# Layer norms by row tile inside the stage that feeds them, and two smaller reorderings, in a two-layer cross-attention kernel on one core

## The chip, the core and the metric

The kernel runs on one core of one Trainium2 chip. Its engines run side by side and are ordered by semaphores alone: TensorE (PE, matrix products), VectorE (DVE), ScalarE (ACT), GpSimd (POOL), and SyncE (SP), whose queue issues all DMAs here. The metric is the device time of one execution in microseconds; lower is better.

## What is computed

Activations `x` of 8 x 112 rows and 512 columns go through two layers, against one context of 8 x 375 rows. All is float32.

```python
# layer 0: 16 heads of 32; layer 1: two attentions of 16 heads of 128, each with one extra key and value
def layer_norm(x, w, b):
    mu = jnp.mean(x, axis=-1, keepdims=True)
    var = jnp.mean(jnp.square(x - mu), axis=-1, keepdims=True)
    return (x - mu) * jax.lax.rsqrt(var + EPS) * w + b
# layer 0
x = x + attention(layer_norm(x, ln1), ctx)            # q, k, v, softmax, output projection
x = x + gelu_tanh(layer_norm(x, ln2) @ fc_w + fc_b) @ proj_w + proj_b      # 512 -> 2048 -> 512
# layer 1
x = x + cross_attention(layer_norm(x, ln1), ctx, ...)  # inner width 2048
x = x + cross_attention(layer_norm(x, ln2), ctx, ...)
x = x + gelu(layer_norm(x, ln_mlp) @ w_fc1 + b_fc1) @ w_fc2 + b_fc2
```

There are five layer norms, here numbered e = 0 to 4: before layer 0's queries (0), before its MLP (1), before the queries of layer 1's two attentions (2 and 3) and before the last MLP (4).

## The kernel before, in words

`x` stays in SBUF as seven row tiles of 128 rows (`RT`). A float32 product is made of three products of halves (`product`, lines 1090 to 1095): every operand is split into a rounded `hi` and a rest `lo`. The normalized and transposed activations are `act_t` (hi and lo). Weights pass through two slots, a and b: a DMA loads a block of 512 x 512 into `w_raw` in four column parts (`load_block`), ScalarE writes the hi part (`split_hi`), GpSimd or VectorE the lo part (`split_lo`), and the next load of a part waits for the lo of the one before.

`schedule` (lines 249 to 275) is the order that every engine follows: norm 0, the first two contexts, queries, attention of layer 0, its projection, norm 1, four MLP blocks, then a hardware loop of two (`a`) with norm 2 + a, contexts, four groups of queries, attention and four groups of projections, then norm 4 and four MLP blocks. Each engine has its own function of each name, and an engine's stream is in order.

**A norm.** The statistics of a row tile are made on VectorE behind the add that finishes it (`add_y`, line 1017, when `last`). `ln_head` (line 834) runs before the add of the last tile: epsilon, one square root on ScalarE for six tiles, reciprocals, normalization (`normalized`, line 829) of tiles 0 and 1 into `prob`. Then `ln` takes the tiles in turn: four transposes on TensorE into one of two PSUM banks (line 1104), scale and bias on ScalarE into one of two `o` buffers (line 596), the two halves on VectorE (lines 861 and 863). Only then come ScalarE's split of the pending weight block (the b slot's block that the previous stage had not split; line 604) and GpSimd's work: it waits for the last half of the last tile (line 502), subtracts the pending block, and adds the bias of the coming projection to `x` (line 507, seven operations), and after that the context halves (line 513).

**Queries** (line 1107): eight tiles per group, t (four column parts) outer and half (448 rows each) inner, into the four banks of `ps_y` in turn; the first tile waits for four row tiles of the norm, the second for all seven. ScalarE writes them into four staging buffers (`staged`: `prob` 0 and 1, `o` 0 and 1), SyncE stores each to a scratch in DRAM, and after each pair loads a part of the block after the next. SyncE's `ln` has the reload of the pending slot ahead of the contexts and of all query stores.

**The MLP** (line 1304): up for rows 0 to 511 and for 512 to 895 (`MLP_CHUNKS`), four tiles of 128 hidden columns each, then down for both, row tile by row tile. **The projection** (line 1282) goes row tile by row tile through the four banks.

## Time and profile before

| what | value |
|---|---|
| median of 3 runs | 2485.12 us (2481.1 to 2485.22) |
| profiled execution, its own time | 2485.79 us |
| its span in the profile | 2484.0 us |
| granted TensorE clock, mean of the span | 0.984 |
| TensorE busy | 2388.7 us (96%) |
| VectorE busy | 1063.9 us (43%) |
| ScalarE busy | 1069.8 us (43%) |
| GpSimd busy | 584.0 us (24%) |
| share of TensorE on the chain that ended last | 81% |

A busy TensorE is not one at its peak: its products are pipelined, and a granted clock of 0.50 means that they run at half speed. A line of the timeline gives the start in microseconds, the length, the engine, the line of the code, the operation, what it writes and reads, its shape, how many were merged into the line, and in brackets the engine's idle time before it with what ended it.

### The profile page before, as it was taken

To read this page: it belongs to the slowest core of one execution; us is meant where nothing else is said; L and a number is where in the kernel's file an instruction comes from. 1 tells how busy PE (TensorE), PEld (TensorE's weight loads), DVE (VectorE), ACT (ScalarE), POOL (GpSimd) and SP (SyncE) were. 2 spreads that over 40 slices of the span, in tenths; PEclk is the share of its full clock that TensorE was granted. 3 is DMA by queue.
4 is the path that set the end of the run, shared out by engine and by line. 5 is a ranking of instruction groups with operands and counts; after the bars stand their busy time and mean duration, and the time that the engine had idled before them with its cause. 6 is when DMAs were issued, how large, how long until landed. Compare 5 with 4: busy or idle time off the path is not lost.

```text
span 2484.0 us, 45212 instructions
## 1 busy us (share of the span) xinstructions
PE 2388.7 (96%) x13858; PEld 2118.2 (85%) x13858; DVE 1063.9 (43%) x2313; ACT 1069.8 (43%) x2551; POOL 584.0 (24%) x975
## 2 busy tenths in 40 slices
PE   6999889999999999999999899999999999999999
PEld 5777678888998998998998798998998998988788
DVE  6777663441333333334334522333333333344633
ACT  3677742243444444444443433444444444452321
POOL 4111023240222222223121230222223122221421
PEclk9999889999999999999999999999999999999999
DMA  6110012244112112112214262113112112215110
GB/s 191 44 34 20 10 48 61 62 131 118 42 57 95 55 44 94 59 49 88 71 58 132 62 187 79 49 50 94 59 42 92 59 61 81 70 51 152 56 51 30
DMA packets 196144, 179.45 MB, mean 72 GB/s; under 512 B 53758, under 2 KB 184242, under 8 KB 196018
## 3 DMA queue, kind: packets, MB, share of 16 engines
q1 hardware_dynamic: 196018, 177.97, 23.4%
q8 instruction: 55, 0.90, 0.2%
q14 instruction: 71, 0.58, 0.1%
HBM read 144.89 MB, written 33.05 MB: 72 GB/s over the span
## 4 chain that ended last, share of the span: by engine, by line
PE 81%; issue 9%; DVE 4%; ACT 3%; POOL 2%; DMA 0%; ACTq 0%; SPq 0%; POOLq 0%; DVEq 0%
PE ps_v L1093 9%; PE ps_v L1095 9%; PE ps_v L1094 9%; PE ps_k L1093 8%; PE ps_k L1095 8%; PE ps_k L1094 8%; PE ps_o L1243 6%; PE ps_s L1093 3%; PE ps_s L1095 3%; PE ps_s L1094 3%; PE ps_o L1093 3%; PE ps_o L1095 3%; PE ps_o L1094 3%; PE ps_t L1232 3%; PE ps_t L1173 1%
## 5 line engine op out<-in xcount | busy, mean ns | idle before, releaser
L513 POOL TENSOR_TENSOR cs_lo<-ctx_raw,cs_hi 128x376 fp32r<-128x376 f32 x288 | 284.5, 1019 | 739.3 <-DVE cs_hi L874 739.3
L969 DVE SCALAR_TENSOR_TENSOR k_lo<-ps_k,col_b,k_hi 128x375 fp32r<-128x375 f32 x256 | 155.6, 608 | 673.2 <-ACT k_hi L696 673.2
L1093 PE MATMUL ps_v<-w_b_hi,cs_hi 128*128 128x512 f32 (+1 forms) x928 | 389.6, 420 | 9.1 <-POOL w_b_lo L497 7.5
L1093 PE MATMUL ps_k<-cs_hi,w_a_hi 128*128 128x376 f32 x1152 | 390.4, 339 | 5.7 <-DVE k_lo L969 4.1
L1095 PE MATMUL ps_k<-cs_hi,w_a_lo 128*128 128x376 f32 x1152 | 385.5, 335 | 0.0
L1094 PE MATMUL ps_k<-cs_lo,w_a_hi 128*128 128x376 f32 x1152 | 385.1, 334 | 0.0
L1095 PE MATMUL ps_v<-w_b_hi,cs_lo 128*128 128x512 f32 (+1 forms) x928 | 365.5, 394 | 0.0
L1094 PE MATMUL ps_v<-w_b_lo,cs_hi 128*128 128x512 f32 (+1 forms) x928 | 365.4, 394 | 0.0
L696 ACT ACTIVATE k_hi<-ps_k,col_b 128x375 fp32r<-128x375 f32 x256 | 146.8, 573 | 423.4 <-PE ps_k L1095 412.3
L713 ACT ACTIVATE prob<-ps_s,row_columns 112x376 f32<-112x376 f32 x256 | 147.1, 574 | 217.9 <-DVE row_columns L975 217.9
L1093 PEld LDWEIGHTS ps_k<-cs_hi,w_a_hi 128*128 128x128 f32 x1152 | 217.2, 189 | 18.9 <-issue 6.2
L1094 PEld LDWEIGHTS ps_k<-cs_lo,w_a_hi 128*128 128x128 f32 x1152 | 217.0, 188 | 10.4
L1095 PEld LDWEIGHTS ps_k<-cs_hi,w_a_lo 128*128 128x128 f32 x1152 | 217.1, 188 | 0.0
L1243 PE MATMUL ps_o<-prob_t,v 128*128 128x112 f32 (+1 forms) x1536 | 211.8, 275 | 0.0
L1243 PEld LDWEIGHTS ps_o<-prob_t,v 128*128 128x128 f32 (+1 forms) x1536 | 209.1, 193 | 0.0
L1095 PEld LDWEIGHTS ps_v<-w_b_hi,cs_lo 128*128 128x128 f32 (+1 forms) x928 | 172.1, 185 | 42.1
L1093 PEld LDWEIGHTS ps_v<-w_b_hi,cs_hi 128*128 128x128 f32 (+1 forms) x928 | 173.5, 187 | 40.3 <-issue 9.6
L625 ACT ACTIVATE v<-ps_v 128x512 f32<-128x512 f32 (+1 forms) x216 | 128.8, 596 | 167.5 <-PE ps_v L1095 167.5
L1094 PEld LDWEIGHTS ps_v<-w_b_lo,cs_hi 128*128 128x128 f32 (+1 forms) x928 | 172.9, 186 | 28.3
L497 POOL TENSOR_TENSOR w_b_lo<-w_raw_b,w_b_hi 128x512 fp32r<-128x512 f32 x84 | 107.6, 1307 | 358.4 <-ACT w_b_hi L582 225.5
L535 POOL CAST k_hi<-xk_hi 128x1 fp32r x256 | 47.8, 187 | 583.7 <-PE ps_s L1095 583.7
L892 DVE TENSOR_SCALAR prob<-prob,row_columns 112x376 f32<-112x376 f32 (+1 forms) x384 | 170.0, 443 | 13.5
(197 smaller groups left out, 4394.0 us busy)
## 6 DMA issues: line engine op xcount, KB each, us to landing
ctx_raw<-in_ctx_t SPq DMA_DIRECT2D x72, 752.0 KB, 5.4
w_raw_a<-in_blocks_a SPq DMA_DIRECT2D x104, 256.0 KB, 3.1
w_raw_b<-in_blocks_b SPq DMA_DIRECT2D x104, 256.0 KB, 3.2
q_lo<-q_scratch SPq DMA_DIRECT2D x72, 224.0 KB, 2.5
o_scratch<-o SPq DMA_DIRECT2D x64, 224.0 KB, 2.0
q_scratch<-prob SPq DMA_DIRECT2D x36, 224.0 KB, 2.6
q_scratch<-o SPq DMA_DIRECT2D x36, 224.0 KB, 2.5
cs_hi<-o_scratch SPq DMA_DIRECT2D x6, 672.0 KB, 4.2
```

Of the source, the lines that this page charges most:

```text
L497: pool.tensor_tensor(w[slot][1][:, :, part], w_raw[slot][:, :, part], w[slot][0][:, :, part], ALU.subtract).then_inc(w_lo[slot], 1)
L513: pool.tensor_tensor(cs[place.parity][1][:, part], ctx_raw[place.parity][:, part], cs[place.parity][0][:, part], ALU.subtract).then_inc(cs ...
L625: act.activation(v[place.parity][0:n, i, :], ps_v[0:n, :], ACT.Identity).then_inc(v_ev, 1)
L696: act.activation(k[t % 2][0][:, 0:LK], ps_k[:, 0:LK], ACT.Identity, bias=col_b[:, ds(place.column((C_BK0, C_BK1), t), 1)]).then_inc(k_hi, 1)
L713: act.activation(prob[buf][0:LQ, 0:KW], ps_s[buf][0:LQ, 0:KW], ACT.Exp, bias=max_neg[0:LQ, buf:buf + 1], accum_out=prob_sum[0:LQ, buf:buf ...
L892: dve.tensor_scalar(p[0:LQ, 0:keys], p[0:LQ, 0:keys], prob_rcp[0:LQ, col:col + 1], None, ALU.mult).then_inc(s_norm, 1)
L969: dve.scalar_tensor_tensor(out=k[t % 2][1][:, 0:LK], in0=ps_k[:, 0:LK], scalar=col_b[:, ds(place.column((C_BK0, C_BK1), t), 1)], in1=k[t % ...
L1093: pe.matmul(out, w_h, m_h, start=first, stop=False)
L1094: pe.matmul(out, w_h, m_l, start=False, stop=False)
L1095: return pe.matmul(out, w_l, m_h, start=False, stop=last)
L1232: last = pe.transpose(ps_t[buf][0:n, i * LQ:(i + 1) * LQ], prob[buf][0:LQ, i * P:i * P + n], ident[0:LQ, 0:LQ])
L1243: last = pe.matmul(ps_o[t % 2][:, 0:LQ], v[place.parity][0:n, i, t * P:(t + 1) * P], prob_t[t % 2][0:n, i * LQ:(i + 1) * LQ], start=(i == ...
```

## The change

Rows pass through the norm while the stage before still runs. Behind a projection (norms 1, 3, 4), the square root, reciprocal and normalization of a row tile follow one row behind the add, the turn of row r - 2 stands behind the products of row r on TensorE, and VectorE's halves stand at the end of each row. Behind the MLP of layer 0 (norm 2), `TURNS_LATE` puts the turns of rows 0 and 1 behind down row 3, of row 2 behind row 4, and so on. In all of them rows 5 and 6 are turned behind the first two tiles of the next stage (the query or the first chunk of up). Queries now go through the first half of the rows with all four column parts, then through the second half, and only tile 4 waits for the whole norm. Normalized rows have buffers of their own (`xhat`). The first norm is done row by row as well, and ScalarE takes over the hi part of the first weight block from GpSimd. On SyncE the pending slot's reload moves from `ln` to behind the fourth query store. ScalarE's split of the pending block moves behind the fourth query tile, or, in the MLP, into the first chunk. Epsilon becomes the bias of the square root. Two inner hardware loops are unrolled (the halves of the query groups, and blocks 0 to 2 of the last MLP).

```diff
@@ -54,6 +54,9 @@
...
+TURNS_LATE = {3: (0, 1), 4: (2,), 5: (3,), 6: (4,)}
@@ -249,29 +253,32 @@
...
-            query(0, 0, 0, 0, A_Q0, 0)
+            query(0, 0, 0, 0, A_Q0, 0, norm=0)
             attend_first()
-            project(0, 0, 0, 1, B_O0, 0, 0)
+            project(0, 0, 0, 1, B_O0, 0, 0, norm=1)
             ln(1, RT)
-            mlp(0, 0, 1, RT)
+            mlp(0, 0, 1, RT, before=1)
             with eng.Fori(1, 3) as fg:
                 mlp(0, fg, 1, RT * (fg + 1))
-            mlp(0, 3, 1, RT * 4, True)
+            mlp(0, 3, 1, RT * 4, norm=2)
             with eng.Fori(0, 2) as a:
                 ln(2 + a, 5 * RT + 4 * RT * a)
                 contexts(ATT1, a)
-                with eng.Fori(0, GROUPS // 2) as half:
+                for half in range(GROUPS // 2):
                     for slot, first in ((0, A_L1), (1, B_L1)):
-                        query(1, a, 2 * half + slot, slot, PER_LAYER * a + half + first, 1 + 4 * a + 2 * half + slot)
+                        group = 2 * half + slot
+                        query(1, a, group, slot, PER_LAYER * a + half + first, 1 + 4 * a + group,
+                              norm=None if group else 2 + a)
                 attend(a)
                 for group in range(GROUPS):
                     slot = group % 2
                     project(1, a, group, slot, PER_LAYER * a + group // 2 + (B_L1 if slot else A_L1) + 6,
-                            1 + 4 * a + group, 5 * RT + 4 * RT * a + RT * group)
+                            1 + 4 * a + group, 5 * RT + 4 * RT * a + RT * group,
+                            norm=3 + a if group == GROUPS - 1 else None)
             ln(4, 13 * RT)
-            with eng.Fori(0, 2) as fg:
+            mlp(1, 0, 4, 13 * RT, before=4)
+            for fg in range(1, 3):
                 mlp(1, fg, 4, 13 * RT + RT * fg)
-            mlp(1, 2, 4, 15 * RT)
             mlp(1, 3, 4, 16 * RT)
 
...
+        def staged_late(i):
+
+            return i in (2, 3)
...
+        def later_rows(norm):
+
+            if norm is None:
+                return {}
+            return {0: (4, 5) if isinstance(norm, int) and norm == 0 else (5,), 1: (6,)}
@@ -358,9 +375,12 @@
                 wait(sp, bias_add, RT * e)
                 sp.dma_start(bias_row[:], row_bias[ds(e, 1), :].partition_broadcast(P)).then_inc(bias_in, 16)
                 sp.sem_inc(sp_waited, 1)
-                if has_pending(e):
-                    slot, n, _ = pending(e)
-                    load_block(slot, n + 1)
+                if isinstance(e, int) and e in (1, 4):
+                    load_pending(e)
+
+            def load_pending(e):
+                slot, n, _ = pending(e)
...
+            def query(layer, a, group, slot, n, step, norm=None):
                 for i in range(2 * NT):
-                    t, half = i // 2, i % 2
+                    t, half = i % NT, i // NT
                     sp.wait_ge(q_act, 8 * step + i + 1)
                     dst = q_scr[ds(group, 1), half * 4:half * 4 + 4, :, t * LQ:(t + 1) * LQ]
                     sp.dma_start(dst.rearrange("o b p r -> p (o b) r"), staged(i).rearrange("p (b r) -> p b r", b=NB // 2))\
                         .then_inc(q_out[i % 4], 16)
+                    if layer and norm is not None and i == 3:
+                        load_pending(norm)
                     if half:
                         load_block(slot, n + 2, [t])
...
-            pool.wait_ge(w_in[0], 16 * NT)
-            for s in range(4):
-                part = slice(s * P, (s + 1) * P)
-                pool.tensor_copy(w[0][0][:, :, part], w_raw[0][:, :, part]).then_inc(w_hi[0], 1)
...
+            def deviation(e, r):
+                act.wait_ge(ln_agg, RT * e + r + 1)
+                act.sem_inc(act_waited, 1)
+                act.activation(std[:, r:r + 1], mean_var[:, r, 1:2], ACT.Sqrt, bias=eps_column[:, 0:1]).then_inc(ln_std, 1)
+
+            def scaled(e, r):
+                act.wait_ge(ln_turn, RT * e + r + 1)
+                wait(act, ln_lo, RT * e + r - 1)
+                act.sem_inc(act_waited, 1)
+                for c in range(DT):
+                    last = act.activation(o[r % 2][:, c * P:(c + 1) * P], ps_t[r % 2][:, c * P:(c + 1) * P], ACT.Identity,
+                                          bias=col_a[:, ds(C_LN + 8 * e + 4 + c, 1)],
+                                          scale=col_a[:, ds(C_LN + 8 * e + c, 1)])
+                last.then_inc(ln_act, 1)
+
+            def split_pending(e, subs):
+                slot, n, products = pending(e)
+                split_hi(slot, n, subs, lambda s: (y_mm, products))
+
             def ln(e, x0):
-                def deviation(part, rows):
-                    act.wait_ge(ln_eps, 2 * e + part + 1)
-                    act.activation(std[:, rows], var_eps[:, rows], ACT.Sqrt).then_inc(ln_std, 1)
-
-                deviation(0, slice(0, RT - 1))
-                for r in range(RT):
-                    act.wait_ge(ln_turn, RT * e + r + 1)
-                    wait(act, ln_lo, RT * e + r - 1)
-                    act.sem_inc(act_waited, 1)
-                    for c in range(DT):
-                        last = act.activation(o[r % 2][:, c * P:(c + 1) * P], ps_t[r % 2][:, c * P:(c + 1) * P], ACT.Identity,
-                                              bias=col_a[:, ds(C_LN + 8 * e + 4 + c, 1)],
-                                              scale=col_a[:, ds(C_LN + 8 * e + c, 1)])
-                    last.then_inc(ln_act, 1)
-                    if r == 0:
-                        deviation(1, slice(RT - 1, RT))
-                if has_pending(e):
-                    slot, n, products = pending(e)
-                    split_hi(slot, n, range(4), lambda s: (y_mm, products))
-                else:
-                    split_hi(1, 0, range(4), None)
...
-            def query(layer, a, group, slot, n, step):
+                if isinstance(e, int) and e == 0:
+                    for r in range(RT):
+                        if 2 <= r < 6:
+                            scaled(0, r - 2)
+                        deviation(0, r)
+                        if r == 4:
+                            split_hi(0, 0, range(4), None)
+
...
                 for i in range(2 * NT):
-                    t, half = i // 2, i % 2
+                    t, half = i % NT, i // NT
                     col = (N_CB1 * a + C_BQ1 if layer else C_BQ0) + NT * group + t
                     act.wait_ge(q_mm, 8 * step + i + 1)
-                    wait(act, q_out[i % 4], 16 * (2 * step + t // 2))
+                    if norm is not None and staged_late(i):
+                        act.wait_ge(ln_lo, RT * norm + RT)
+                    wait(act, q_out[i % 4], 16 * (2 * step + half))
                     act.sem_inc(act_waited, 1)
                     act.activation(staged(i), ps_y[i % 4][:, 0:HALF], ACT.Identity, scale=scale,
                                    bias=(col_b if layer else col_a)[:, ds(col, 1)]).then_inc(q_act, 1)
+                    for row in later_rows(norm).get(i, ()):
+                        scaled(norm, row)
+                    if norm is not None and i == 3:
+                        if layer:
+                            split_pending(norm, range(4))
+                        else:
+                            split_hi(1, 0, range(4), None)
                     if half:
-                        split_hi(slot, n + 1, [t], lambda s: (q_mm, 8 * step + 2 * s + 2))
+                        split_hi(slot, n + 1, [t], lambda s: (q_mm, 8 * step + NT + s + 1))
...
+                for r in range(RT if norm is not None else 0):
+                    if r >= 2:
+                        scaled(norm, r - 2)
+                    deviation(norm, r)
@@ -789,9 +825,19 @@
...
                                        bias=col_a[:, ds(col, 1)]).then_inc(h_act, 1)
+                        for row in later_rows(before).get(f, ()) if c == 0 else ():
+                            scaled(before, row)
+                        if c == 0 and before is not None and f >= 2:
+                            split_pending(before, (2 * f - 4, 2 * f - 3))
+                for r in range(3 if norm is not None else 0):
+                    deviation(norm, r)
                 split_hi(0, na + 1, range(4), lambda s: (h_mm, HIDDEN * (4 * m + fg) + HIDDEN - 4 + s + 1))
-                if not last:
+                if norm is None:
                     split_hi(1, nb + 1, range(4), lambda s: (y_mm, x0 + RT))
+                for r in range(3, RT if norm is not None else 0):
+                    deviation(norm, r)
+                    for row in TURNS_LATE[r]:
+                        scaled(norm, row)
...
+            def halves(e, r):
+                z = o[r % 2][:].rearrange("p (k n) -> p k n", k=DT)
+                dve.wait_ge(ln_act, RT * e + r + 1)
+                dve.tensor_copy(act_t[0][:, :, r * P:(r + 1) * P], z).then_inc(ln_hi, 1)
+                dve.wait_ge(ln_hi, RT * e + r + 1)
+                dve.tensor_tensor(act_t[1][:, :, r * P:(r + 1) * P], z, act_t[0][:, :, r * P:(r + 1) * P],
+                                  ALU.subtract).then_inc(ln_lo, 1)
...
+                        if r:
+                            reciprocal_deviation(0, r - 1)
+                        statistics(0, r)
+                        if r:
+                            normalized(0, r - 1)
+                        mean_variance(0, r)
+                        if 2 <= r < 6:
+                            halves(0, r - 2)
+                    reciprocal_deviation(0, RT - 1)
+                    normalized(0, RT - 1)
+                    for r in (4, 5, 6):
+                        halves(0, r)
                     split_lo(1, 0, range(4))
-
-            def query(layer, a, group, slot, n, step):
...
+            def add_and_normalize(r, e, x0, norm, ready):
+
+                add_y(r, e, x0)
+                if r:
+                    reciprocal_deviation(norm, r - 1)
+                dve.wait_ge(x_add, x0 + r + 1)
+                statistics(norm, r)
+                if r:
+                    normalized(norm, r - 1)
+                mean_variance(norm, r)
+                for row in ready:
+                    halves(norm, row)
+
+            def norm_tail(norm, ready):
+                reciprocal_deviation(norm, RT - 1)
+                normalized(norm, RT - 1)
+                for row in ready:
+                    halves(norm, row)
...
+                        if before is not None and (c, f) == (0, 0):
+                            halves(before, RT - 1)
...
+                        if norm is not None and r == 3:
+                            for row in (0, 1):
+                                reciprocal_deviation(norm, row)
+                                normalized(norm, row)
+                        if norm is not None and r > 2:
+                            add_and_normalize(r, e, x0, norm, TURNS_LATE.get(r - 1, ()))
+                            continue
+                        add_y(r, e, x0)
+                        if norm is not None:
+                            dve.wait_ge(x_add, x0 + r + 1)
+                            statistics(norm, r)
+                            mean_variance(norm, r)
...
+            def turn_row(e, r):
+                pe.wait_ge(ln_xhat, RT * e + r + 1)
+                wait(pe, ln_act, RT * e + r - 1)
+                if isinstance(e, int) and e == 0:
+                    pe.wait_ge(vec_ev, 4)
+                for c in range(DT):
+                    last = pe.transpose(ps_t[r % 2][:, c * P:(c + 1) * P], xhat[r % 2][:, c * P:(c + 1) * P], ident[:])
+                last.then_inc(ln_turn, 1)
...
+                    t, half = i % NT, i // NT
+                    if t == 0 and norm is not None:
+                        pe.wait_ge(ln_lo, RT * norm + (RT if half else -(-HALF // P)))
                     pe.wait_ge(w_lo[slot], 4 * n + t + 1)
                     wait(pe, q_act, 8 * step + i - 3)
...
+                    for row in later_rows(norm).get(i, ()):
+                        turn_row(norm, row)
...
+                    if norm is not None and r >= 2:
+                        turn_row(norm, r - 2)
...
+                        for row in later_rows(before).get(f, ()) if c == 0 else ():
+                            turn_row(before, row)
...
+                        for row in TURNS_LATE.get(r, ()) if norm is not None else ():
+                            turn_row(norm, row)
```

## Rows read from the trace of the kernel before

**Rows 1.** The page, part 1: busy time, share of the span, instructions.
```profile
PE 2388.7 (96%) x13858; PEld 2118.2 (85%) x13858; DVE 1063.9 (43%) x2313; ACT 1069.8 (43%) x2551; POOL 584.0 (24%) x975
```

**Rows 2.** Waits of TensorE, whole span: us in total, times, longest us.
```profile
PE ps_t L1104 <- DVE prob L831: 32.3, 26, 10.9
```

**Rows 3.** Timeline of TensorE around norm 2: start us, length us, engine, line, operation.
```profile
504.42 0.39 PE L1095 MATMUL ps_o<-w_b_hi,cs_lo 128*128 128x512 f32 x1
...
507.99 0.63 PE L1104 MATMUL ps_t<-ident,prob 128*128 128x128 f32 x4 [1.62 <-ACT o L596]
...
515.16 0.72 PE L1093 MATMUL ps_k<-act_t_hi,w_a_hi 128*128 128x448 f32 x1
...
519.72 0.36 PE L1093 MATMUL ps_v<-act_t_hi,w_a_hi 128*128 128x448 f32 x1
```

**Rows 4.** Two stretches of norm 2; the granted clock (PEclk) stands behind POOL.
```profile
504.70:509.00 4.30, 1.83 (x13) 1.28 (x12) 3.96 (x10) 2.65 (x9) 0.00 (x0) 1.00 0.00 0
510.00:519.00 9.00, 7.78 (x26) 6.20 (x27) 7.50 (x15) 8.62 (x23) 0.45 (x1) 0.50 0.00 1
```

**Rows 5.** Timeline of TensorE around norm 1.
```profile
338.75 0.39 PE L1095 MATMUL ps_o<-w_b_hi,act_t_lo 128*128 128x512 f32 x1
...
349.14 0.78 PE L1093 MATMUL ps_s<-act_t_hi,w_a_hi 128*128 128x512 f32 x1
...
352.79 0.40 PE L1093 MATMUL ps_s<-act_t_hi,w_a_hi 128*128 128x512 f32 x1
```

**Rows 6.** Timeline of TensorE around norm 3.
```profile
1408.32 0.39 PE L1095 MATMUL ps_o<-w_b_hi,act_t_lo 128*128 128x512 f32 x1
...
1421.32 0.72 PE L1093 MATMUL ps_k<-act_t_hi,w_a_hi 128*128 128x448 f32 x1
...
1424.53 0.37 PE L1093 MATMUL ps_k<-act_t_hi,w_a_hi 128*128 128x448 f32 x1
```

**Rows 7.** Timeline of TensorE around norm 4.
```profile
2314.79 0.39 PE L1095 MATMUL ps_o<-w_b_hi,act_t_lo 128*128 128x512 f32 x1
...
2325.27 0.78 PE L1093 MATMUL ps_s<-act_t_hi,w_a_hi 128*128 128x512 f32 x1
```

**Rows 8.** Timeline of VectorE: two adds of the projection, one row of norm 1.
```profile
333.74 0.69 DVE L1023 TENSOR_TENSOR x<-ps_k,x 128x512 f32<-128x512 f32 x1 [1.22 <-PE ps_k L1095]
...
336.46 0.69 DVE L1023 TENSOR_TENSOR x<-ps_v,x 128x512 f32<-128x512 f32 x1 [1.22 <-PE ps_v L1095]
...
346.26 0.54 DVE L831 TENSOR_SCALAR prob<-x,mean_var,row_columns 128x512 f32<-128x512 f32 x1
346.71 0.42 DVE L861 CAST act_t_hi<-o 128x512 fp32r<-128x512 f32 x1
347.17 0.69 DVE L863 TENSOR_TENSOR act_t_lo<-o,act_t_hi 128x512 fp32r<-128x512 f32 x1
```

**Rows 9.** Timeline of ScalarE: first table load, one row's scaling, one weight split.
```profile
13.45 1.28 ACT L588 ACT_TABLE_LOAD   x1 [13.45 <-DVE row_columns L822]
...
340.33 1.50 ACT L596 ACTIVATE o<-ps_t,col_a 128x128 f32<-128x128 f32 x4 [1.66 <-PE ps_t L1104]
...
351.02 2.20 ACT L582 ACTIVATE w_b_hi<-w_raw_b 128x512 fp32r<-128x512 f32 x4
```

**Rows 10.** Timeline of VectorE: a subtraction while GpSimd works (352 to 369).
```profile
356.54 1.66 DVE L1052 TENSOR_TENSOR cs_lo<-prob,cs_hi 128x512 fp32r<-128x512 f32 x1
```

**Rows 11.** Timeline of the start: VectorE, TensorE and GpSimd.
```profile
8.91 1.29 DVE L811 BATCH_NORM_STATS2 stats<-x 128x6 f32<-128x512 f32 x2 [2.74 <-DMA x<-in_x]
...
30.77 0.72 PE L1093 MATMUL ps_k<-act_t_hi,w_a_hi 128*128 128x448 f32 x1
...
34.10 12.34 POOL L507 TENSOR_TENSOR x<-x,bias_row 128x512 f32<-128x512 f32 x7 [5.95 <-DVE act_t_lo L863]
...
46.40 9.05 POOL L513 TENSOR_TENSOR cs_lo<-ctx_raw,cs_hi 128x376 fp32r<-128x376 f32 x8
...
52.22 0.39 PE L1093 MATMUL ps_v<-w_b_hi,cs_hi 128*128 128x512 f32 x1
```

124 lines of the change are left out of this document (47 added, 77 removed).

## The prediction

> **What bounds the kernel now.** I read the page first: TensorE is busy for 96% of the span [rows 1], so only its idle time and its slow time can be won. Then the list of who waited for whom: the largest of TensorE's waits is for the normalized rows at the turns of the five layer norms, 32.3 us in 26 waits [rows 2]. Then the timeline of TensorE around each norm. The reader should take three times from it: the last product of the projection or MLP before the norm, the first product after it, and the product from which the pitch is the short one again.
>
> At norm 2 the last product starts at 504.42 (a product's place is 0.23 long, so the array is free at 504.65), the next real product at 515.16: 10.5 us, in which only seven row turns of four transposes run. Those first products stand about 0.38 apart, and from the twelfth after the first (519.72) the pitch is 0.20: 4.56 us where 2.43 would do, so 2.1 us more are lost [rows 3]. The granted clock says the same: 1.00 (the 2.4 GHz level) up to 509, 0.50 (1.2 GHz) from 510 to 519, after five microseconds in which the engine only turned rows and waited [rows 4]. A turn at the high level takes 0.63 from first start to last end [rows 3]; the next instruction can begin before that end, so I take 0.5. Seven are 3.5 us, and they stay. What can be won is 10.5 + 2.1 - 3.5 = 9.1 us at norm 2.
>
> The same sum: norm 1, 338.98 to 349.14 is 10.2, plus 1.6 slow (nine products in 3.65 against 9 x 0.227), minus 3.5: 8.3 [rows 5]. Norm 3, 1408.55 to 1421.32 is 12.8, plus 1.4 (nine in 3.21 against 1.82), minus 3.5: 10.7 [rows 6]. Norm 4, 2315.02 to 2325.27 is 10.25, plus 1.7 (the mean of the three), minus 3.5: 8.4 [rows 7]. All four: 36.5 us. Norm 0 stands at the start and is worked out alone.
>
> **Norms 1, 3 and 4 (behind a projection).** The change gives VectorE, per row: add, statistics, normalization, aggregate, reciprocal, the two halves of a row turned earlier. By the distance of one start to the next, halves 0.46 and 0.61 and normalization 0.45 [rows 8]; add and statistics, 0.69 long like the subtraction, 0.7 and 0.6; the two short ones 0.2 each: 3.2 us. TensorE's row was 2.72 (add to add) [rows 8] and is 2.72 + 0.5 = 3.22 with a turn. So the two are level; the four output banks give slack of three rows. I charge 0.5 us a norm, 1.5 in all (bounds 0 and 5). ScalarE has 1.50 us of scaling [rows 9] and a square root of 0.2 per row: covered. Its table load, 1.28, falls behind row 0's aggregate, as the first load of the kernel fell behind its wait [rows 9]; row 0's reciprocal is wanted only 2.7 us later. The Trainium skill (ScalarE: Activation LUTs, What ACT_TABLE_LOAD costs) puts a switch of sets at about 2.66 us with a drain; this would delay row 0's reciprocal by 1.4, still inside a row, and leaves the sum alone except at norm 0 (+1 us).
>
> The first four rows are in halves 0.1 to 0.3 us after the last row's products end, while TensorE turns row 4; the next stage starts at once. Rows 5 and 6 turn behind its first and second tile. In the query, tile 4 needs all rows. After the start Q, tiles 0 and 1 end at 2.4 and 5.4, row 6 is turned at 5.9, scaled by 7.6, in halves by 8.8, and tile 4 comes at 10.8: covered by 2 us. In the MLP the second chunk comes at 12 and the halves are there at about 10. Behind them GpSimd (which waits for the whole norm) subtracts the pending block, four of about 1.3 us (between 9.05/8 and 12.34/7 of its other operations [rows 11]), from Q + 12 at the earliest: done by Q + 17.5 to 19, wanted at Q + 20.4 by query group 1. Its reload and stores 4 to 7 queue behind that on the DMA queue of SyncE; ScalarE wants the first of these stores landed only at Q + 23, and TensorE runs four tiles ahead of it. The stores of tiles 0 to 3 now pass ahead of the reload; no wait of TensorE hangs on them in either order. In the MLP the pending split on ScalarE (2.2 us for four [rows 9]) stands in the first chunk's four up tiles (4 x 2.7 = 10.9 us) with two scalings (3.0) and four activations (near 0.7 each, 2.8): 8.0 us, so it is covered. I cost these at nothing; if the cover of the pending block is gone, it is up to 5 us each at norms 2 and 3. Norm 3 has one thing more: its gap is 2.5 us longer than the others [rows 5 to 7], and it alone holds the jump back of the outer loop, so I lay the 2.5 to code fetched after the jump. The jump stays. TensorE's own share of it is not shown; between 0 and 2.5 I take 0.5, near the low end, since the jump now falls where VectorE and ScalarE have slack. For the unrolled inner loops I take nothing: the list of waits has none that belongs to a loop's head. Gains: 8.3 + 10.2 + 8.4 - 1.5 = 25.4.
>
> **Norm 2 (behind the MLP).** Here the turns of rows 0 and 1 wait for the fourth down row, and VectorE must catch up. From the end of down row 0: row 3 ends at 8.2, turns 0 and 1 by 9.8; ScalarE does row 3's square root before it scales row 0 (to 12.5 or 14.2), and the turn of row 2 needs that bank, so TensorE waits 0.6 to 1.7. VectorE does halves of rows 0 and 1 after row 4 (to 16.2 or 16.9), of row 2 at 19.5 or 20.9, of row 3 at 22.8 or 24.2. TensorE has turned row 4 by 19.4 or 21.2 and waits another 3 to 3.5 for row 3. The later times have GpSimd at work beside VectorE, since the three square roots now stand ahead of the weight split, which so starts 8 us after row 0 and not at once. In the old order the queries began at 16.3 + 10.5 = 26.8 with all rows turned; now at 23 to 24.3 with 1 us of turns to come: 1.5 to 2.9 earlier, and 2.1 of low clock saved if it stays up. Idle of 3.5 us may bring the clock down: the row of four at 507.99 still ran fast 3.3 us after the last product, and by 510 the level was low [rows 3, 4], so it is an even chance, 0 or about 2. Gain 3 (bounds 0 and 6).
>
> That neighbour is a rule against this change. In the trace a VectorE subtraction beside GpSimd takes 1.66 us against 0.69 alone [rows 8, 10]. The Trainium skill (SBUF — State Buffer, Who interferes with whom) explains it: the two share a port pair as an exclusive lock, and a VectorE operation with two SBUF inputs or in a two-port mode fully blocks against it. By that rule the add from PSUM and the statistics go unharmed; only normalization and halves pay, about 1 us each, and it would take norm 2's gain to 1.5.
>
> **Norm 0 (the start).** First products came at 30.77, the norm was whole at 34.10, GpSimd added the bias in 12.34 and split the first context in half of 9.05; that gives 51.0, and attention began at 52.22 [rows 11]. Now: x is there at 8.9 [rows 11]; row 0's root at 11.3 (table load included), then VectorE ends halves 0, 1, 2, 3 at 16.7, 19.2, 21.9 and, with ScalarE's split of the first weights (2.2 [rows 9]) in between, 26 to 28. So queries start 3 to 4.5 us earlier. But rows 4 to 6 are turned behind tiles 0 and 1, the first at the low clock (4.4 us): Q + 4.4, turns 5.4, tile 1 7.9, turn 8.4, scaling 10, halves 11.3. The norm is whole at 37.3 to 39, not 34.1, and GpSimd's bias rows and context come after it: 39 + 12.3 + 4.5 = 56 with its old pace, 53 with 1.35 a row. TensorE ends its queries at about 50.5 and waits. So attention starts 1 to 4 us later than 52.2, take 2.5, and the wait may cost clock (0 to 2, take 1): loss 3.5, bounds +1 gained and 6 lost.
>
> **The sum.** 25.4 + 3 - 3.5 = 24.9 us. The profiled execution took 2485.79 (span 2484.0), 0.7 above the median 2485.12. 2485.8 - 24.9 = 2461.
>
> **The rivals.**
> - A, the forecast: 2461, own range 2454 to 2468.
> - B, all is hidden, norm 2 too: 26.9 + 6 + 1 = 34, 2451. For it: at norm 2 the stall is a sum of small steps that I laid end to end. Against: the order at norm 0 and GpSimd's 17 us.
> - C, VectorE becomes the bound in the projections: its row is level with TensorE's, and each semaphore step I left out lengthens it. At 0.5 us a row over 5 rows and 4 norms, 10 us: 2471.
> - D, the stall moves into the queries: the pending block is late at norms 2 and 3, 5 us each: 2471. The change would then not do what it says for two norms.
> - E, slower: the turns make TensorE wait once a row in the projections, and this broken flow brings the clock down there. Products at 0.43 in place of 0.23 cost 84 x 0.2 = 17 us a projection. It decides from 125 slow products on (25 us); in two of the four stages it gives 2461 + 34 = 2495. For it: the level fell within 5 us of turns and waits [rows 4]. Against: the products between two turns are 2.7 us dense, and waits of VectorE's size there are tenths.
>
> **How the numbers follow.** A 0.60, B 0.12, C 0.14, D 0.07, E 0.07. The likeliest gives 2461. The range takes in B and C and D with the bounds at norms 0 and 2: 2451 to 2473. A measurement tells about 0.2%, 5 us. Faster by more: A, B and nearly all of C and D, 0.91; within: 0.03; slower: 0.06.
>
> **What would show it.** In the profile after: TensorE's waits at turns at norms 1, 3 and 4 under 1 us each, and granted clock 1.00 through these stretches; a wait of 3 to 4 us ahead of the first query product at norm 2 for the halves of row 3; at the start, products from 26 to 28, then a wait of 3 to 5 us ahead of the first value product, ended by GpSimd's context halves. Wrong would be: a low clock inside a projection (E), waits of half a microsecond at every row (C), or a wait for w_b ahead of query group 1 (D).

## The result, and the profile after

| | median, us | runs | against the kernel before beside it |
|---|---|---|---|
| kernel before | 2485.17 (2481.1 to 2485.36) | 4 | |
| changed kernel | 2459.11 (2457.61 to 2463.31) | 4 | 0.9899 [0.9887, 0.9911] |

The change wins 26 us, 1.0%. The profiled execution of the changed kernel took 2459.99, its span is 2458.1, its mean granted clock 0.989. The page's line of busy time, to set beside [rows 1], and then the list of TensorE's waits, whose line for the norms answers to [rows 2]:

```profile
PE 2372.5 (97%) x13858; PEld 2109.3 (86%) x13858; DVE 1064.3 (43%) x2329; ACT 1078.4 (44%) x2579; POOL 580.7 (24%) x971
```
```profile
PE ps_t L1172 <- DVE xhat L871: 11.8, 4, 7.8
PE ps_k L1162 <- DVE act_t_lo L879: 9.2, 2, 6.4
...
PE ps_v L1162 <- POOL cs_lo L535: 5.9, 1, 5.9
...
PE ps_k L1162 <- issue: 2.4, 1, 2.4
```

The 32.3 us of waits for normalized rows are 11.8 now, and those four waits all end by 20.2 us, at norm 0, where no stage runs ahead that could hide them. New in the list are two waits for halves ahead of query products (6.4 at norm 0, 2.9 at norm 2), one for GpSimd's context halves, and one that ends with no releaser ("issue").

**Norms 1, 3 and 4.** TensorE's timeline through norm 1, behind the projection [rows 5 before], shows seven turns with no bracket behind them, so no idle time, 3.19 us apart. The two stretches below give TensorE's busy time and then its granted clock: 0.95, whose low part lies before 327, at the head of the projection and before the first turn, and then 1.00 with TensorE busy throughout. The third fence has the turns and first products of the same norm in the kernel before, at 0.51.

```profile
333.40 0.60 PE L1172 MATMUL ps_t<-ident,xhat 128*128 128x128 f32 x4
336.59 0.60 PE L1172 MATMUL ps_t<-ident,xhat 128*128 128x128 f32 x4
339.77 0.60 PE L1172 MATMUL ps_t<-ident,xhat 128*128 128x128 f32 x4
...
352.52 0.60 PE L1172 MATMUL ps_t<-ident,xhat 128*128 128x128 f32 x4
```
```profile
324.00:345.00 21.00, 21.00 (x106) 0.95 0.26 76
345.00:351.00 6.00, 6.00 (x32) 1.00 0.01 3
```
```profile
342.00:352.00 10.00, 7.87 (x27) 0.51 0.01 2
```

**Norm 2.** Behind the MLP two waits are left, and the first query tile runs slowly: from 507.75 to the next turn at 512.39 are 4.6 us, and the stretch around it has a clock of 0.66. The same places of the kernel before are in [rows 3].

```profile
497.88 0.63 PE L1172 MATMUL ps_t<-ident,xhat 128*128 128x128 f32 x4 [1.27 <-ACT o L613]
...
507.75 0.74 PE L1162 MATMUL ps_k<-act_t_hi,w_a_hi 128*128 128x448 f32 x1 [2.87 <-DVE act_t_lo L879]
...
512.39 1.05 PE L1172 MATMUL ps_t<-ident,xhat 128*128 128x128 f32 x4
```
```profile
505.00:511.00 6.00, 3.25 (x9) 0.66 0.28 119
```

**Norm 0.** At the start the order costs time. TensorE, VectorE and GpSimd of the changed kernel up to the first value product, which stood at 52.22 before [rows 11]:

```profile
27.64 0.74 PE L1162 MATMUL ps_k<-act_t_hi,w_a_hi 128*128 128x448 f32 x1 [6.36 <-DVE act_t_lo L879]
...
56.81 0.77 PE L1162 MATMUL ps_v<-w_b_hi,cs_hi 128*128 128x512 f32 x1 [5.94 <-POOL cs_lo L535]
```
```profile
42.78 5.99 DVE L853 TENSOR_TENSOR w_b_lo<-w_raw_b,w_b_hi 128x512 fp32r<-128x512 f32 x4 [3.60 <-ACT w_b_hi L600]
48.69 2.88 DVE L910 CAST cs_hi<-ctx_raw 128x1504 fp32r<-128x1504 f32 x2
```
```profile
39.32 10.60 POOL L529 TENSOR_TENSOR x<-x,bias_row 128x512 f32<-128x512 f32 x7 [12.29 <-DVE act_t_lo L879]
50.80 10.00 POOL L535 TENSOR_TENSOR cs_lo<-ctx_raw,cs_hi 128x376 fp32r<-128x376 f32 x8 [0.88 <-DVE cs_hi L910]
```

VectorE's split of `w_b` comes 8.9 us later than in the kernel before. Some 5 us of this are the later norm. The other 3.6 are the bracket above: VectorE waits for ScalarE's half of the same weights, which the change has put behind the fourth query tile. In the kernel before, the split followed the norm at once, and the context's cast was ready before GpSimd came to it:

```profile
33.88 5.80 DVE L807 TENSOR_TENSOR w_b_lo<-w_raw_b,w_b_hi 128x512 fp32r<-128x512 f32 x4
39.60 3.97 DVE L874 CAST cs_hi<-ctx_raw 128x1504 fp32r<-128x1504 f32 x2
```

Behind its wait TensorE has two slow stretches, where the kernel before ran at 1.00. They cost 2.8 us more: the distance between the two kernels grows from 4.6 us at this product to 7.4 at 108.

```profile
57.00:62.00 5.00, 5.00 (x18) 0.72 0.82 235
72.00:78.00 6.00, 6.00 (x38) 0.72 0.00 0
```

**Where the 25.9 us of the two spans lie.** Three kinds of instructions stand at the same place of the work in both kernels: the first value product of each attention (52.22 and 56.81 for the first, then those below) and the last GELU ahead of norm 2. Kernel before, then changed kernel, TensorE and ScalarE:

```profile
485.87 0.58 ACT L789 ACTIVATE prob<-ps_s,col_a 128x384 f32<-128x384 f32 x1 [1.50 <-PE ps_s L1095]
597.44 0.50 PE L1093 MATMUL ps_v<-w_b_hi,cs_hi 128*128 128x512 f32 x1
1504.35 0.50 PE L1093 MATMUL ps_v<-w_b_hi,cs_hi 128*128 128x512 f32 x1
```
```profile
482.00 0.58 ACT L825 ACTIVATE prob<-ps_s,col_a 128x384 f32<-128x384 f32 x1 [1.50 <-PE ps_s L1164]
591.64 0.49 PE L1162 MATMUL ps_v<-w_b_hi,cs_hi 128*128 128x512 f32 x1
1488.51 0.49 PE L1162 MATMUL ps_v<-w_b_hi,cs_hi 128*128 128x512 f32 x1
```

The table has these places and four more, products of TensorE that both timelines have (their tiles stand in the first column). Each stretch begins where the one above it ends.

| stretch, up to | before | changed | difference of the stretch | predicted, charges included |
|---|---|---|---|---|
| norm 0 and the slow products behind it (`ps_s<-k_hi,q_hi`) | 100.86 | 108.24 | +7.4 | +3.5 (2.5 + 1 of clock) |
| attention of layer 0 (`ps_v<-w_b_lo,act_t_hi`) | 324.25 | 329.54 | -2.1 | 0 |
| norm 1 and the MLP, to the last GELU | 485.87 | 482.00 | -9.2 | -7.8 (-8.3 + 0.5) |
| norm 2, to the next value product | 597.44 | 591.64 | -1.9 | -3 |
| first attention of layer 1 (`ps_v<-w_a_hi,act_t_lo`) | 1384.52 | 1377.06 | -1.7 | 0 |
| norm 3, to the third value product | 1504.35 | 1488.51 | -8.4 | -9.7 (-10.2 + 0.5) |
| second attention of layer 1 (`ps_k<-w_b_lo,act_t_hi`) | 2298.24 | 2281.48 | -0.9 | 0 |
| norm 4, to the end | 2484.0 | 2458.1 | -9.1 | -7.9 (-8.4 + 0.5) |

So 4.7 of the 25.9 us lie outside the norms. The 2.1 in the attention of layer 0 go with the granted clock of its last 40 us, 0.66 in the kernel before (285 to 325) and 0.73 in the changed one. They can't be credited to the change: e9 below, with the code of the kernel before in this stretch, passed it 1.5 us faster than that kernel did.

In layer 1's attentions something else is gone. In the kernel before ScalarE stands four times, some 3 us each, with no releaser, twice in each attention and 182 us apart, which is one turn of the loop over head groups (line 290 of the kernel before). At these four places together the changed kernel gains 2.9 us on TensorE (it gives 0.3 back at the end of the second attention):

```profile
ACT prob_t L707 <- issue: 12.8, 4, 3.6
```
```profile
803.18 0.45 ACT L707 ACTIVATE prob_t<-ps_t 128x336 f32<-128x336 f32 x1 [3.65 <-issue]
```

No run of the changed kernel or of its variants has these waits, and e9, the kernel before with SyncE's order alone edited, still has all four (12.1 us). So they go with the change, though no part of it touches this loop. Which part does it no run shows; the unrolled inner loops, which change ScalarE's code ahead of it, are one candidate.

### The profile page after: what moved, and what is told of

Its sections match the earlier page's. It is cut to its first block, busy times and chain, and to the rows that moved or that the text cites. A ratio compares the mean times of both kernels' runs of the same rounds, so it can differ in the third digit from the quotient of the medians.

```text
span 2458.1 us, 44941 instructions
## 1 busy us (share of the span) xinstructions
PE 2372.5 (97%) x13858; PEld 2109.3 (86%) x13858; DVE 1064.3 (43%) x2329; ACT 1078.4 (44%) x2579; POOL 580.7 (24%) x971
## 4 chain that ended last, share of the span: by engine, by line
PE 85%; issue 7%; ACT 3%; POOL 2%; DVE 2%; DMA 0%; POOLq 0%; ACTq 0%; SPq 0%; DVEq 0%
PE ps_v L1162 9%; PE ps_v L1163 9%; PE ps_v L1164 9%; PE ps_k L1162 9%; PE ps_k L1164 9%; PE ps_k L1163 9%; PE ps_o L1318 6%; PE ps_s L1164 4%; PE ps_s L1162 4%; PE ps_s L1163 4%; PE ps_o L1164 3%; PE ps_o L1162 3%; PE ps_o L1163 3%; PE ps_t L1307 3%; PE ps_t L1248 1%
## 5 line engine op out<-in xcount | busy, mean ns | idle before, releaser
L1162 PE MATMUL ps_v<-w_b_hi,cs_hi 128*128 128x512 f32 (+1 forms) x928 | 390.9, 421 | 15.1 <-POOL w_b_lo L519 7.6
```

Of the source, the lines that this page charges most:

```text
L1162: pe.matmul(out, w_h, m_h, start=first, stop=False)
```

## The experiments

All times are medians. Each group of runs had the kernel before beside it on its chip. The changed kernel, run again in the second group, is what the edits are compared with; as the groups differ a little, both columns count.

| run | group | us | ratio to before, 95% |
|---|---|---|---|
| e1_context_first | 1 | 2452.39 | 0.9873 [0.9858, 0.9888] |
| e2_mlp_as_projection | 1 | 2453.38 | 0.9876 [0.9861, 0.9891] |
| e3_outer_unrolled | 1 | 2455.53 | 0.9887 [0.9872, 0.9902] |
| e4_reload_first | 1 | 2480.67 | 0.9986 [0.9977, 0.9995] |
| after_again | 2 | 2458.81 | 0.9894 [0.9879, 0.9910] |
| e5_norm0_whole | 2 | 2455.21 | 0.9877 [0.9862, 0.9892] |
| e6_extra_statistics | 2 | 2464.06 | 0.9913 [0.9898, 0.9928] |
| e8_reload_behind_contexts | 2 | 2465.92 | 0.9924 [0.9910, 0.9938] |
| e7_all_three | 3 | 2442.61 | 0.9830 [0.9817, 0.9843] |
| e9_before_stores_first | 3 | 2485.49 | 1.0004 [0.9995, 1.0013] |

### SyncE's order: nothing by itself, 22 us for the rest of the change

**e4_reload_first** puts the reload back into SyncE's `ln`:

```diff
-                if isinstance(e, int) and e in (1, 4):
+                if has_pending(e):
                     load_pending(e)
...
-                    if layer and norm is not None and i == 3:
-                        load_pending(norm)
```

> The changed kernel, with SyncE's reload of the pending slot back ahead of the contexts and all query stores at norms 2 and 3. The prediction held that no wait of TensorE hangs on this order: within 1 us. Rival, read from the trace after: the pending block is split only at 528.3 (20.6 us behind the first query product), so the first stores would be issued at about 529 and landed at 532, ScalarE's fifth tile waits for them, and TensorE's ninth tile (531.3) waits for ScalarE: 1 to 3 us at each of the two norms, 2 to 6 us slower.

Measured: 2480.67, 22 us over the changed kernel. The order matters far more than the expectation and its rival had it: nearly the whole gain of the change is gone. The trace of this run at norm 2, SyncE's queue, then ScalarE, then TensorE with the bracket of its wait, and the stretch behind it (norm 3 repeats it with a wait of 8.54 us):

```profile
523.44 4.28 SPq L371 DMA_DIRECT2D w_raw_b<-in_blocks_b  x4
527.95 0.96 SPq L389 DMA_DIRECT2D ctx_raw<-in_ctx_t  x2
529.07 1.82 SPq L404 DMA_DIRECT2D q_scratch<-prob  x2
```
```profile
537.28 0.63 ACT L639 ACTIVATE prob<-ps_k,col_b 128x448 f32<-128x448 f32 x1 [13.84 <-DMA q_scratch<-prob]
```
```profile
537.97 0.74 PE L1160 MATMUL ps_k<-act_t_hi,w_b_hi 128*128 128x448 f32 x1 [7.55 <-ACT prob L639]
```
```profile
535.00:541.00 6.00, 3.03 (x8) 0.53 0.70 176
```

Read backwards: TensorE stands 7.55 us because all four result buffers are full; ScalarE, which empties them, stands 13.84 us for a staging buffer whose store has not landed; that store, of a tile that ScalarE had written at 512.5, was issued at 529.07, because SyncE's in-order stream stood at the reload, which waits for GpSimd's low halves of the pending block, and these come late now that ScalarE splits the block only behind the fourth query tile. In the changed kernel the same four stores leave from 513.55 on. After the wait TensorE runs at the low level (0.53). The two waits are 16.1 us, and the span is 20.5 longer; the slow stretches behind the waits are the likely rest.

**e8_reload_behind_contexts** puts the reload ahead of the stores but behind the two context transfers:

```diff
+                if layer and norm is not None:
+                    load_pending(norm)
                 for i in range(2 * NT):
...
-                    if layer and norm is not None and i == 3:
-                        load_pending(norm)
```

> The reload of the pending weights is issued ahead of the query stores again at norms 2 and 3, as in the run that took 2480.7 us, but behind the two transfers of contexts and not ahead of them. In that run ScalarE's fifth query copy waited 13.8 us for the landing of the first query store, and TensorE 7.6 and 8.5 us for that copy. Theory: two things added up there, that the store stands behind SyncE's wait for GpSimd's low halves (issued at 529.1 where it was 513.6), and that it stands behind two context transfers of 752 KB each (8.2 us to landing). With the contexts out of its way the store lands some 4 us after its issue at 528, ScalarE copies at 532, and TensorE, which comes to its stop at 530.4, waits 2 to 3 us at either norm: 2464 to 2469 us. Rival: the semaphore wait alone does it, and the time stays at 2480. Second rival: the contexts alone did it, and the time is that of the changed kernel, 2459.

Measured: 2465.92, as the theory had it. TensorE's waits for ScalarE at norms 2 and 3, the second row from norm 3:

```profile
533.97 0.52 PE L1162 MATMUL ps_k<-act_t_hi,w_b_hi 128*128 128x448 f32 x1 [2.36 <-ACT prob L641]
...
1434.44 0.48 PE L1162 MATMUL ps_k<-act_t_hi,w_b_hi 128*128 128x448 f32 x1 [2.17 <-ACT prob L641]
```

The stores were issued at 529.24, as late as in e4, and behind the same four parts of the reload (256 KB each). Their median time to landing was 4.3 us (2.5 to 4.7). In e4, with two transfers of 752 KB as well, issued a microsecond earlier, it was 8.1 (7.9 to 8.6). So the late issue costs about 7 us in all and the two transfers ahead in the queue 15 more. The Trainium skill (DMA: Bandwidth & Descriptors, Two DMAs through the same engine are not ordered) says that the descriptors of one queue start in order though they need not finish so; the doubled time to landing agrees with it.

**e9_before_stores_first** makes the same move in the kernel before (SyncE's two halves written out, so that the first group can be told apart):

```diff
-                if has_pending(e):
-                    slot, n, _ = pending(e)
-                    load_block(slot, n + 1)
+                if isinstance(e, int) and e in (1, 4):
+                    load_pending(e)
...
+                    if layer and isinstance(group, int) and group == 0 and i == 3:
+                        load_pending(2 + a)
```

> The kernel before with nothing changed but SyncE's order at norms 2 and 3: the reload of the pending weights is issued behind query store 3, as the change has it. In the kernel before ScalarE waits 22.7 us in all for landings of query stores, and TensorE never for ScalarE there: GpSimd splits the pending block ahead of the queries, so the reload is issued 5 us behind the first query product, the first query store 11 us behind it, and TensorE has four result buffers. Theory: the order is worth nothing where the pending block is split early, and is only needed once that split is late (with the old order the changed kernel took 2480.7): within 1.5 us of the kernel before, about 2484.5, with ScalarE's waits for the stores gone or much smaller. Rival: the stores' order is a gain of its own that the changed kernel merely keeps, then 2465 to 2478.

Measured: 1.0004 [0.9995, 1.0013], no difference, though ScalarE's waits for the stores fell from 22.7 us (12 waits) to 1.7 (one). The list of waits of ScalarE, kernel before, then this run:

```profile
ACT o L616 <- DMA q_scratch<-o: 11.4, 6, 5.3
ACT prob L616 <- DMA q_scratch<-prob: 11.3, 6, 4.9
```
```profile
ACT o L626 <- DMA q_scratch<-o: 1.7, 1, 1.7
```

In the kernel before the four result buffers swallowed waits of 5 us; in the changed kernel with the old order they could not swallow 13.8. The move of the stores wins nothing; it is what lets the pending block be split late.

### The start: VectorE and GpSimd side by side

**e1_context_first** lets GpSimd split the first contexts ahead of norm 0's bias rows:

```diff
             def ln(e, x0):
+                if isinstance(e, int) and e == 0:
+                    contexts(ATT0, 0, True)
                 pool.wait_ge(ln_lo, RT * e + RT)
```

> The changed kernel, with GpSimd's halves of the first two contexts ahead of its wait for norm 0 and its bias rows. My theory: the 5.9 us that TensorE waits at the start for GpSimd's context halves come from the order on GpSimd (10.6 us of bias rows stand ahead) and from VectorE's subtractions beside it (5.99 us for four). Without them VectorE ends the four by about 45.6, the first context's hi by 47, GpSimd's halves by about 52, and the first value product starts at 52 and not at 56.8; the low clock behind the wait goes too (1.5 to 2). So 6 to 7 us less than the changed kernel, near 2453. Rival: VectorE's own chain (first halves, then the weight block) is what ends last; then the value product moves by under 2 us and the time by under 2.

Measured: 2452.39, 6.4 under the changed kernel (by the ratios 5.2). The first value product stands at 51.74 with a wait of 1.43. What moved is seen on VectorE, whose split and cast now have GpSimd idle beside them (42.78 5.99 and 48.69 2.88 in the changed kernel):

```profile
42.23 2.50 DVE L857 TENSOR_TENSOR w_b_lo<-w_raw_b,w_b_hi 128x512 fp32r<-128x512 f32 x4 [3.60 <-ACT w_b_hi L604]
44.65 1.79 DVE L914 CAST cs_hi<-ctx_raw 128x1504 fp32r<-128x1504 f32 x2
```

GpSimd's bias rows had slowed the two VectorE steps that the context halves wait for, by 3.5 and 1.1 us. The edit takes this away and GpSimd's own lateness with it. By an estimate each is about half: with its order kept but no VectorE work beside it, GpSimd would have ended its seven rows at 39.32 + 8.75 (e5 below) = 48.1. Its context halves began at 50.80 in the changed kernel and at 45.73 here.

**e5_norm0_whole** turns all seven rows ahead of the queries again, with the weight split left where the change has it:

```diff
-                    for r in range(4):
+                    for r in range(RT):
                         turn_row(0, r)
```

> Norm 0 is turned whole again: all seven row tiles ahead of the first query product, and none inside the queries; everything else as in the changed kernel, also the place of the weight splits. Theory: at norm 0 the spreading of the rows wins nothing, because the first value product waits for GpSimd's low half of the contexts, which waits for VectorE's weight split and cast, and those come after query tile 3. TensorE then starts the queries some 5 us later (about 33 where it was 27.6), goes through them without a stop, and meets the first value product at 56 to 58 with a wait of 2 us or less in place of 5.9: the time stays within 2 us of the changed kernel, about 2459. Rival: spreading the rows itself is what delays the contexts (the kernel before had its first value product at 52.2), so that undoing it gives the 4.6 us back, about 2454. Second rival: the 5 us of later start are lost in full, 2464.

Measured: 2455.21, 3.6 under the changed kernel (by the ratios 4.2). This is near the first rival and outside the theory. GpSimd's bias rows come at 34.46, they are over before VectorE's split begins, and this takes 2.50 us as in e1:

```profile
34.46 8.75 POOL L531 TENSOR_TENSOR x<-x,bias_row 128x512 f32<-128x512 f32 x7 [7.58 <-DVE act_t_lo L883]
```
```profile
54.26 0.47 PE L1166 MATMUL ps_v<-w_b_hi,cs_hi 128*128 128x512 f32 x1 [1.24 <-POOL cs_lo L537]
```

The expectation had the queries start some 5 us later, at 33, with VectorE's split behind their fourth tile. They start at 31.1, take less time with no turns inside, and the split starts at 44.74, only 2.0 later than in the changed kernel; it and the cast are then 4.6 us shorter without GpSimd beside them. The clock stays at 1.00 too (0.71 in the changed kernel from 50 to 57). Spreading norm 0 over the queries is thus a loss of some 4 us as the change does it. With GpSimd's order turned round (e1) the first value product comes earlier than here, 51.74 against 54.26. No run turns the order round with norm 0 whole, or puts ScalarE's split of `w_b` back ahead of the queries (VectorE waits 10.42 us for it here), so whether the spreading itself pays is open.

### Norm 2 behind the MLP

**e2_mlp_as_projection** gives the MLP ahead of norm 2 the order of the projections, row r - 2 turned behind down row r, in place of `TURNS_LATE`:

```diff
-                        for row in TURNS_LATE.get(r, ()) if norm is not None else ():
-                            turn_row(norm, row)
+                        if norm is not None and r >= 2:
+                            turn_row(norm, r - 2)
```

> The changed kernel, with norm 2 done like norms 1, 3 and 4: turn of row r - 2 behind down row r, halves in the same VectorE row, ScalarE's weight split ahead of all square roots. My theory: the waits at norm 2 (1.3 for a bank of turned rows, 2.9 ahead of the first query product) and the slow products behind them (4.6 us for the first tile where 2.4 do) come from the late turns alone: 6 us less, near 2453, with TensorE's waits there under 1 us. Rival: GpSimd's split beside VectorE in rows 0 and 1, and VectorE's row as long as TensorE's, keep a stall of the same size: under 2 us less.

Measured: 2453.38, 5.4 under the changed kernel (by the ratios 4.5). No turn and no query product waits, and the clock stays up where it was 0.66:

```profile
504.53 0.60 PE L1162 MATMUL ps_t<-ident,xhat 128*128 128x128 f32 x4
507.59 0.60 PE L1162 MATMUL ps_t<-ident,xhat 128*128 128x128 f32 x4
```
```profile
505.00:511.00 6.00, 6.00 (x35) 1.00 0.14 40
```

### The jump back of the outer loop

**e3_outer_unrolled** writes the loop of two out:

```diff
-            with eng.Fori(0, 2) as a:
+            for a in range(2):
```

> The changed kernel, with the outer hardware loop over the two attentions of layer 1 written out twice. My theory: the wait of 2.36 us ahead of the first query product at norm 3, which nothing in the profile releases, is TensorE fetching code behind the loop's jump back; without a jump it goes, and the time falls by 2.4 us, near 2457. Rival: the code is fetched as late in a straight line, or the longer program costs elsewhere; then nothing, or slower by 1 to 5 us.

Measured: 2455.53, 3.3 under the changed kernel; by the ratios 1.7, and the intervals overlap, so the time alone does not settle it. The trace does. The changed kernel has this wait at the head of norm 3's queries, and e3 has no wait of TensorE there:

```profile
1405.95 0.46 PE L1162 MATMUL ps_k<-act_t_hi,w_a_hi 128*128 128x448 f32 x1 [2.36 <-issue]
```

In e3 the same product starts at 1400.47, right behind the one before it. Part of e3's gain is elsewhere: its first query product stands at 26.53 and not 27.64, which nothing in the edit explains.

### How close VectorE is to the bound

**e6_extra_statistics** adds one statistics instruction per row, unused, at all norms but norm 2:

```diff
+                if not (isinstance(norm, int) and norm == 2):
+                    dve.bn_stats(stats_x[:, r, :], x[:, r, :])
```

> One more statistics instruction of VectorE (0.6 us by those of the trace, its result unused) for each row tile of norms 0, 1, 3 and 4, none at norm 2. In the projections VectorE's row took 3.19 us without any idle time, and TensorE's row 3.19 as well. Theory: the two are level there, so each added 0.6 us comes out as a wait of TensorE, for 5 to 7 rows in three norms: 9 to 12 us and 1 to 2 at the start, 2469 to 2473; the granted clock stays at 1.00 in the projections. Rival: VectorE has slack that its being always busy hides (it fills up, ahead of TensorE), then under 3 us in all, 2459 to 2462. Second rival: waits that come each row bring TensorE's low clock in the projections, then some 17 us more for each of the three, 2500 and over.

Measured: 2464.06, 5.3 more, between the theory (2469 to 2473) and its rival (2459 to 2462). VectorE's rows are now 3.50 apart (3.19 before the edit), so 0.6 us of work lengthened the row by 0.31:

```profile
339.10 0.69 DVE L1058 TENSOR_TENSOR x<-ps_o,x 128x512 f32<-128x512 f32 x1
...
342.61 0.68 DVE L1058 TENSOR_TENSOR x<-ps_k,x 128x512 f32<-128x512 f32 x1
```

So VectorE had 0.3 us of slack in each row: a row of its own work is 2.9 us and TensorE's is 3.19, and TensorE is the bound by that much. TensorE's new waits are one of 0.5 to 0.6 us in each of the three projections and one of 0.47 ahead of the next stage at norms 1 and 4. Its granted clock is 1.00 from the first turn to the end of each of the three projections, so these waits did not bring rival E of the prediction about; but this edit makes at most two of them a norm, not one a row. At norm 3 the clock falls behind the wait at the outer loop's jump, 3.5 us in this run (0.82 from 1406 to 1413).

### All three together

**e7_all_three** joins the edits of e1, e2 and e3.

> The three edits that each won alone, together: GpSimd splits the first contexts ahead of norm 0's bias rows (6.4 us against the changed kernel's 2458.8), the MLP step ahead of norm 2 turns its rows like a projection (5.4), and the outer loop is written out twice (3.3). They touch three different places of the time line (start, norm 2, norm 3), so theory: they add up, 2458.8 less 15.1 is 2443.7, expected 2442 to 2446. Rival: what one of them wins at norm 2 or at the start was only moved there and is won once (the later row turns and the unrolled program both shift the code around norm 2), then 2447 to 2450.

Measured: 2442.61, ratio 0.9830 [0.9817, 0.9843]: 42 us under the kernel before and 16 under the changed kernel. The single gains add up by the medians (15.1). By the ratios they are 11.4 against 15.9, which tells how well such differences are known. Its list of TensorE's waits has neither the context halves nor the "issue" any more, and the wait for halves at norm 2 is gone; what is left of the norms is the start:

```profile
PE ps_t L1166 <- DVE xhat L873: 12.3, 4, 8.3
...
PE ps_k L1156 <- DVE act_t_lo L881: 5.2, 1, 5.2
```

**after_again**, the yardstick of the second group:

> The changed kernel itself, unedited, beside the edits of this group and on the same chip, so that small differences are taken against it and not against another day's runs. Expected 2457 to 2461 us. If it came out at 2454 to 2456, the gains of about 6 us read so far for the context split ahead of the bias rows and for the MLP turned like a projection would shrink to 2 to 4 us.

Measured: 2458.81, so the gains stand as they were read.

## Why the prediction was right, and where it was not

The time came out 2 us from the forecast, by case A. At each norm the gain or loss has the sign that was forecast, but the closeness is luck. By the table above, the norms are off by +3.9, -1.4, +1.1, +1.3 and -1.2 us (together +3.7), and 4.7 us were won in the attentions, for which the forecast had no term: -1.0 in sum. Norm 0's loss of 7.4 lies outside its own bounds (6 lost at most).

- **Norms 1, 3 and 4: right.** -9.2, -8.4 and -9.1 against terms of -8.3, -10.2 and -8.4. The reading behind them, that the gap less seven turns is what can be won and that the low clock goes with the gap, holds: no wait at a turn, clock 1.00. Norms 1 and 4 won 0.9 and 0.7 more than the terms. A turn costs 0.47 (a row of 3.19 against 2.72) and not 0.5, which gives 0.2 of it; the rest stays open.
- **The charge of 1.5 us for VectorE in the projections: not needed.** The prediction had VectorE at 3.2 a row and TensorE at 3.22. The row of 3.19 is right, but by e6 VectorE has 0.3 us of slack in it. Rival C was rightly taken as near: 0.6 us a row brought waits at once.
- **The jump back: undersized.** TensorE's own share was taken as 0.5 of 2.5 "since the jump now falls where VectorE and ScalarE have slack". It is 2.36, and the slack of other engines did not shorten it. This is norm 3's miss: 10.7 less 2.36 is 8.3, and 8.4 were won.
- **The unrolled inner loops: taken at nothing** because "the list of waits has none that belongs to a loop's head". TensorE's list has none. ScalarE's has the 12.8 us shown above, at the jumps of a loop that the change leaves alone, and TensorE lost 2.9 us by them. That the unrolling took them away is not shown.
- **Norm 2: right in kind, too large.** The forecast had a wait of 0.6 to 1.7 for a bank and 3 to 3.5 ahead of the first query; they are 1.27 and 2.87. The clock was called an even chance, worth 0 or about 2, and it fell: 0.66 here, 0.72 in e3. In e6, behind the same wait of 2.87, it stayed at 1.00. So -1.9, and not -3. What the prediction left out is that the stall was a choice of the order, not of the MLP: e2 shows none.
- **Norm 0: right in sign, too small.** The first products were to come at 26 to 28 (27.64), the norm to be whole at 37.3 to 39 (39.2), GpSimd to follow. The step that failed is "56 with its old pace, 53 with 1.35 a row". GpSimd's bias rows took 10.6 us, 1.5 a row, and were done at 49.9. Then came two terms that the sum has not or has too small. The contexts began only at 50.80, because VectorE's cast came only then: its chain started late behind ScalarE's half of `w_b`, and the bias rows slowed it. And from there to the first value product it took 6.0 us, not 4.5. The slow products behind the wait cost 2.8 us where 1 was taken (0 to 2); in after_again, the same kernel, they cost 1.6. The prediction named the contention of VectorE and GpSimd for norm 2 and did not apply it to VectorE here. The rule of the Trainium skill that it cited (SBUF — State Buffer, Who interferes with whom) fits in kind: 0.62 us a split alone, 1.5 beside GpSimd (e1 against the changed kernel), and also e5's bias rows, 8.75 where they had no split beside them. The drain that the prediction allowed for behind the table load does not show here: the load took 1.28 us from 9.95, and the square root began at 11.25.
- **SyncE's order: the step that was wrong.** "No wait of TensorE hangs on them in either order" is true of the kernel before (e9) and false of the changed one (e4, 22 us). The prediction followed the new order, found it free, and did not ask what the old order would do with the pending block split later: GpSimd is done with it 20.6 us behind the first query product at norm 2, where it was 8.4. It followed the reload forward to stores 4 to 7 but not, for the old order, to stores 0 to 3. As the change has the good order, the time was not touched.
- **Rival D** (pending block late): GpSimd was done at 528.3, that is Q + 20.6 where 17.5 to 19 was said and Q + 20.4 wanted; no wait of TensorE came of it.

## What to carry to other kernels

Moving work out of a gap into the stage before is worth the gap less the work itself, plus the slow products behind the gap; both can be read off before the change. Whenever a step is made later, follow each in-order queue that waits for it, and count what stands behind that wait: four small stores behind one late reload and two large transfers cost 22 us. An order that looks harmless, such as bias rows on GpSimd, can be dear through the engine beside it, so compare the length of the same instruction with and without its neighbour. And before a time is called explained, match the same products in both timelines stage by stage: here a sum within 2 us hid misses of up to 4.

## What the runs showed of the hardware that was not expected

- A wait of 2.36 us (2.2 to 3.5 over the runs with the loop) with no releaser stands on TensorE behind the jump back of a loop body of some 900 us, and is gone when the loop is written out. That it is the fetching of instructions is an argument, not shown.
- ScalarE stood 2.9 to 3.7 us with no releaser at four jumps back of a loop of 182 us, in the kernel before and in e9, and at none in the changed kernel, whose attention code is the same. So such a wait can come or go with a change elsewhere in the program.
- A store of 224 KB landed in 4.3 us behind four transfers of 256 KB in the same queue, and in 8.1 us with two of 752 KB between.
- VectorE's subtraction of 128x512 took 0.62 us alone and 1.5 us beside GpSimd's additions, and its cast of 128x1504 0.9 against 2.0 (3.97 for two in the kernel before); GpSimd's seven additions took 8.7 us alone, 10.6 with the split beside them, and 12.3 in the kernel before, with splits and casts beside all of them.
